# Three blocks of 384 tokens in tiles of 128 instead of four of 288 in tiles of 96, attention units in rings of their own, and the product with v by a block diagonal

## The chip, the cores and the metric

One core of one Trainium2 chip. The time is the device time of one execution, in microseconds (us); a kernel's time is the median of its runs. The engines are TensorE (PE, with its weight loads listed apart as PEld), VectorE (DVE), ScalarE (ACT), GpSimd (POOL) and SyncE (SP), which here only issues DMAs.

## The reference

A vision tower of depth 1 on 32 images of 3 x 96 x 96: 36 patches an image, so 1,152 tokens of 192 features.

```python
h = tok(x)                                  # patches -> 5 mixtures of channels -> 192 features, plus biases
h = h + attn(layernorm(h), W_qkv, W_out)    # 12 heads of 64 within an image; logits are q k * 8
h = h + ffn(layernorm(h), gate, w1, b1, w2, b2)
# ffn: argmax over 8 experts; out = gelu(xt @ w1[e] + b1[e]) @ w2[e] + b2[e], hidden size 768
```

All is fp32 in and out. The choice of the expert depends on the exact logits of the gate, so the kernel splits factors of q, k and v into a high and a low part in fp32r.

## The kernel before

**Tiling.** The 1,152 tokens go in NB = 4 blocks of BT = 288, each of NT = 3 tiles of TT = 96. A unit of attention is two images, GT = 72 tokens, so a block has NU = 4 units and starts and ends on whole images: block, tile group and unit never cross. Everything indexed by block, `h`, `qT`, `kT`, `probs`, `rows`, `v`, is a buffer for one block.

**Stages of a block b** (PE's program, `body`, which handles the tokens of b + 1 between the attention of b): `tokens` (the six products of x with the effective patch weights, a tile at a time; L413), `turn_xn` (two transposes of the normalised tile; L421, L422), `heads` (q and k of a pair of heads for the whole block, five products of 128 weight columns by 288 tokens; L428), `values` (v of a tile, two halves of 384 columns, five products each with the tokens stationary; L428), `scores` (24 small products for a unit; L458), `turn_probs` (24 small products with the identity; L472), `attend` (probabilities with v, 24 products of 36 x 64 weights by 36 columns; L487), `project` (output projection of a tile; L498), `gate` (L513, L514), `ranks` (L529 to L538: place of each token among those of its expert), and at the end `first_lists` and `more_lists`, which turn the ranks into lists of token numbers. Fp32 products are two instructions each, fp32r ones a single one; `keep_clock` (L556) are filler transposes.

**Softmax of a unit.** `scores` fills two PSUM banks, which it waits for until DVE has run `soften` of the unit before (maximum, L1027, subtraction, L1028); ACT takes the exponential (L840); DVE runs `normalise` (sum, reciprocal, product; L1036 to L1038); PE turns the probabilities (`turn_probs`), ACT copies them out of PSUM (`take_probs`, L857, one copy), PE runs `attend`, ACT copies the result (`take_attended`, L863). `turn_probs(g + 1)` waits for the copy of g, `attend(g)` too. DVE's order is written out in `soften_all` and `body`.

**v.** ACT copies a tile's values to SBUF, SP moves them by DMA (L382) to partitions 0 to 35 for one image of a unit and 64 to 99 for the other; a run of tokens that lies in one image and one tile is one DMA, 40 in all.

**Order around it.** PE, ACT and DVE each have an order written out by hand; PSUM banks 0 to 3 are a ring of results of `heads`, `values`, `tokens`, `project` and the transposes, whose order stands in `OPENING`, `MIDDLE` and `FINAL`. The last block overlaps with nothing: its four units' attention, three projections, gates and ranks stand in a row, and behind them the lists, the gather of the tokens, and the experts: 16 tiles of 128 gathered tokens, `up` (L738, L744), `down` (L764). SP loads x block by block into `xb`, all of w1 at once, and w2 in three pieces of experts.

## Time and profile before

| | |
|---|---|
| median of 3 runs | 268.12 us (265.56 to 268.46) |
| the profiled execution | 268.89 us, span 267.0 |
| PE busy | 253.0 us, 95% |
| PE weight loads | 235.1 us, 88% |
| DVE, ACT, POOL busy | 131.2, 114.7, 55.8 us |
| mean granted clock of TensorE | 0.974 |

Busy time of PE counts overlapped matmuls once, and their listed durations reach from issue to the modelled end: the cost of one is the step to the next start. The span is the time from the first instruction to the last on the core; the device time lies 1.9 us above it.

### The profile page before, as it was taken

Reading aid. Unit: us, or ns where it says so; the run is one execution under the profiler, and the core shown is the slowest. Engines: PE = TensorE matmul, PEld = TensorE weight load, DVE = VectorE, ACT = ScalarE, POOL = GpSimd, SP = SyncE. Lnnn points to the kernel's source line nnn. Section 1 sums busy time; section 2 is a strip of 40 time slices with the busy share of each in tenths; the row PEclk is TensorE's granted clock in tenths of the full one; section 3 lists DMA queues with packets and bytes.
Section 4 is the critical chain, followed back from the end, with each engine's and each line's share of the span. In section 5 each row is a group of like instructions: output and inputs, shape, how many; then the busy total and the mean of one; then the engine's idle time right before and its main releaser. Section 6 shows DMA issues by size and latency. Waiting matters only on the chain.

```text
span 267.0 us, 9115 instructions
## 1 busy us (share of the span) xinstructions
PE 253.0 (95%) x3855; PEld 235.1 (88%) x3855; DVE 131.2 (49%) x422; ACT 114.7 (43%) x309; POOL 55.8 (21%) x97
## 2 busy tenths in 40 slices
PE   7999999999999999989999989889999999999990
PEld 6999889999899999779999879888899999999990
DVE  3786387331596731786731793267242423232310
ACT  2866552525343525432525443240342547475420
POOL 3020002122002122002124000125234444443222
PEclk9999999999999999999999975999999999999997
DMA  6939982313631306421005411022211211222000
GB/s 227 310 103 305 433 294 72 101 39 99 239 87 49 136 2 178 189 60 47 6 0 184 124 48 49 1 69 62 87 35 52 72 63 61 62 53 68 3 3 0
DMA packets 8019, 27.17 MB, mean 102 GB/s; under 512 B 2085, under 2 KB 3777, under 8 KB 7468
## 3 DMA queue, kind: packets, MB, share of 16 engines
q1 hardware_dynamic: 5820, 22.02, 25.1%
q0 software_dynamic: 1840, 4.13, 5.7%
q8 instruction: 31, 0.51, 0.8%
q10 hardware_dynamic: 320, 0.44, 0.6%
q14 instruction: 8, 0.07, 0.1%
HBM read 20.40 MB, written 3.34 MB: 89 GB/s over the span
## 4 chain that ended last, share of the span: by engine, by line
PE 90%; DVE 5%; issue 2%; ACT 1%; POOL 1%; POOLq 0%; DVEq 0%
PE psum L428 20%; PE psum L764 12%; PE psum L498 10%; PE psum L738 8%; PE psum L413 7%; PE psum L472 6%; PE psum L487 5%; PE psum L744 5%; PE psum L556 3%; PE psum L458 3%; PE psum L584 2%; PE psum L567 2%; PE psum L727 2%; PE psum L421 1%; PE psum L514 1%
## 5 line engine op out<-in xcount | busy, mean ns | idle before, releaser
L428 PE MATMUL psum<-xn_hi,wq_parts 128*128 128x288 f32 x144 | 34.4, 308 | 0.3 <-DVE late_r L1004 0.3
L764 PE MATMUL psum<-w2s,kT 128*128 128x192 f32 (+1 forms) x192 | 33.8, 327 | 0.0
L1344 POOL TENSOR_SCALAR veps<-mv 96x1 f32<-96x1 f32 x21 | 4.6, 217 | 133.3 <-DVE mv L985 133.3
L764 PEld LDWEIGHTS psum<-w2s,kT 128*128 128x128 f32 x192 | 30.8, 190 | 0.1
L428 PE MATMUL psum<-late_r,wq_parts 128*128 128x288 f32 x96 | 27.4, 294 | 0.0
L498 PE MATMUL psum<-wo,oT 128*96 128x192 f32 x144 | 27.1, 340 | 0.0
L1403 POOL DMA_INDIRECT out<-oT,ids x16 | 16.2, 1010 | 43.7 <-DVE oT L1300 43.7
L428 PEld LDWEIGHTS psum<-xn_hi,wq_parts 128*128 128x128 f32 x144 | 24.4, 188 | 0.5 <-ACT xn_hi L826 0.5
L960 ACT ACTIVATE kT<-psum,w1s 128x128 f32<-128x128 f32 x48 | 13.3, 375 | 26.3 <-PE psum L744 26.3
L498 PEld LDWEIGHTS psum<-wo,oT 128*96 128x96 f32 x144 | 23.6, 171 | 0.5
L428 PE MATMUL psum<-wq_parts,xn_hi 128*96 128x384 f32 x72 | 22.2, 363 | 0.0
L1282 DVE COPY qT<-psum 128x128 f32<-128x128 f32 x16 | 4.7, 292 | 34.5 <-PE psum L728 34.5
L960 ACT ACTIVATE kT<-psum,late 128x128 f32<-128x128 f32 x48 | 13.3, 376 | 16.7 <-PE psum L744 11.2
L472 PEld LDWEIGHTS psum<-ident,kT 36*36 36x36 f32 x768 | 16.1, 122 | 3.7 <-DVE kT L1038 1.7
L848 ACT COPY wq_in<-psum 96x384 f32<-96x384 f32 x24 | 11.3, 473 | 17.8 <-PE psum L428 17.8
L413 PE MATMUL psum<-late,xb 128*96 128x192 f32 x108 | 18.8, 329 | 0.0
L472 PE MATMUL psum<-ident,kT 36*36 36x36 f32 x768 | 17.9, 206 | 0.8 <-DVE kT L1038 0.8
L428 PEld LDWEIGHTS psum<-late_r,wq_parts 128*128 128x128 f32 x96 | 18.1, 188 | 0.0
L1392 POOL DMA_INDIRECT xb<-token_table,ids x16 | 15.6, 976 | 9.9 <-DVE ids L1222 5.3
L413 PEld LDWEIGHTS psum<-late,xb 128*96 128x96 f32 x108 | 17.2, 163 | 0.2
L835 ACT COPY kT<-psum 128x288 f32<-128x288 f32 x24 | 9.6, 400 | 16.8 <-PE psum L428 16.8
L487 PE MATMUL psum<-late 36*64 36x36 f32 x768 | 16.1, 233 | 0.7 <-issue 0.7
(165 smaller groups left out, 481.1 us busy)
## 6 DMA issues: line engine op xcount, KB each, us to landing
w1s<-w_b SPq DMA_DIRECT2D x1, 4632.0 KB, 18.2
xb<-xT SPq DMA_DIRECT2D x4, 864.0 KB, 5.7
w2s<-w SPq DMA_DIRECT2D x2, 1728.0 KB, 8.9
late<-wq_in SPq DMA_DIRECT2D x24, 108.0 KB
token_table<-rows SPq DMA_DIRECT2D x3, 432.0 KB, 3.3
w2s<-w SPq DMA_DIRECT2D x1, 1152.0 KB, 7.4
late<-w_proj SPq DMA_DIRECT2D x2, 480.0 KB, 3.9
b2s<-b SPq DMA_DIRECT2D x1, 768.0 KB
```

The costliest lines, as they stand in the source:

```text
L413: mm = pe.matmul(dst[0:TT, 0:D], xb[:, k, t * TT:(t + 1) * TT], weff[:, k // 2, k % 2, :], start=(k == 0), stop=(k == KX - 1))
L428: mm = pe.matmul(dst, lhsT, rhs, start=(i == 0), stop=(i == len(parts) - 1))
L472: mm = pe.matmul(psum[image, TR_BANK, cols], probs[image, g, cols], ident[image, image], start=True, stop=True)
L487: mm = pe.matmul(psum[DH * k:DH * (k + 1), SIDE_BANKS[i], at:at + PER_IMAGE], v[image, g, col:col + DH], probsT[image, g % 2, j * PER_IMAG ...
L498: mm = pe.matmul(dst[0:TT, 0:D], oT[:, c, t * TT:(t + 1) * TT], wo[:, c, :], start=(c == 0), stop=(c == PAIRS - 1))
L738: pe.matmul(psum[:, 2 * p2 + c % 2, at:at + SLOT], w[:, c * P:(c + 1) * P], fxA[p2], start=(c < 2), stop=False)
L744: mm = pe.matmul(psum[:, 2 * p2 + c % 2, at:at + SLOT], w[half, FF + at:FF + at + P], fxB[p2][half, :], start=False, stop=(c >= FCH - 2))
L764: mm = pe.matmul(psum[:, Y_BANKS[j % 2], 0:D], hidT[j % 2][:, c * P:(c + 1) * P], w[:, :, c, :], start=(c == 0), stop=(c == FCH - 1))
L848: cp = act.copy(v_tiles[:, t, f * (HD // 2):(f + 1) * (HD // 2)], acc(slot[0])[0:TT, 0:HD // 2])
L960: ge = act.activation(hidT[p2][:, c * P:(c + 1) * P], psum[:, 2 * p2 + c % 2, c // 2 * P:(c // 2 + 1) * P], ACT.Gelu, bias=w1_of(j)[:, UP ...
L1392: pool.indirect_dma_start(out=xg[j % 4], out_offset=None, in_=table, in_offset=bass.IndirectOffsetOnAxis(ap=ids[:, j:j + 1], axis=0)).then ...
L1403: pool.indirect_dma_start(out=out, out_offset=bass.IndirectOffsetOnAxis(ap=ids[:, j:j + 1], axis=0), in_=yo[j % 4], in_offset=None, bounds ...
```

## The change

**Blocks.** `NB` is 3, `TT` 128: a block has 384 tokens in three tiles, nine tiles in all (`TILES`), and its product for q and k has 384 columns. 384 is not a multiple of 72, so a unit, an output row tile and a block no longer coincide. Units run from 0 to 15 through the kernel; a block has 5, 5 and 6 of them (`UNITS`), and finishes the row tiles whose last unit it has: 2, 3 and 4 (`GROUPS`). Their buffers become rings: `v` of 6 units, `probs` of 4, `h` of 7 tiles (which makes `hres`, the copy kept for the residual, superfluous), `rows` and what turns it of 4 tiles. `qT` and `kT` hold 432 tokens, so that from block 1 on a q or k product is copied in two pieces.

**Product with v.** The turned probabilities of a unit's two images are laid into a block diagonal of 100 partitions by 12 x 72 columns, whose other blocks POOL sets to zero once (together with the gap between the images in `v`). One product of all 100 partitions then serves both images. It goes into the ring of banks 0 to 3, no longer into the banks of the scores. ACT copies the probabilities in two pieces, one for each image.

**Order.** `PRODUCTS` lists all results in one row. The last block is written out anew: its six units' scores, softmax, turning and products with v stand between its own values. Every middle stage of scores has five units, the fifth behind the last value product. **Memory and DMA.** x lies in the place of w1's experts 6 and 7, which are loaded after the last block of x; the effective patch weights, the low parts and one block diagonal lie in w2's experts 5 to 7, so w2 comes in four pieces. x comes by tiles. POOL's indirect warm-up goes to `bias`. Before the experts, the transpose of the second gathered tile moves ahead of `up(0)`.

```diff
-NB = 4
+NB = 3
-TT = 96
+TT = 128
-NU = BT // GT
+NU = TOKENS // GT
-W2_PIECES = [slice(0, 3), slice(3, 6), slice(6, EXPERTS)]
+W2_PIECES = [slice(0, 3), slice(3, 5), slice(5, 7), slice(7, EXPERTS)]
+V_SLOTS, P_SLOTS, H_SLOTS, ROW_SLOTS = 6, 4, 7, 4
+UNITS = [range(b * BT // GT, (b + 1) * BT // GT) for b in range(NB)]
+GROUPS = [[t for t in range(TILES) if last_unit(t) in units] for units in UNITS]
...
+            def attend(u):
+                slot = product("at", u)
+                dst = into(slot)
+                pe.wait_ge(tr_free, u + 2)
+                values_here(pe, u)
                 for c in range(PAIRS):
                     for k in range(2):
-                        for i in range(GROUP):
-                            image = slice(HALF * i, HALF * i + PER_IMAGE)
-                            mm = pe.matmul(psum[DH * k:DH * (k + 1), SIDE_BANKS[i], at:at + PER_IMAGE],
-                                           v[image, g, col:col + DH],
-                                           probsT[image, g % 2, j * PER_IMAGE:(j + 1) * PER_IMAGE],
+                        j = 2 * c + k
+                        mm = pe.matmul(dst[DH * k:DH * (k + 1), c * GT:(c + 1) * GT],
+                                       v[0:SPAN, u % V_SLOTS, j * DH:(j + 1) * DH],
+                                       probsT[u % 2][:, j * GT:(j + 1) * GT],
                                            start=True, stop=True)
...
+            def take_probs(u):
+                act.wait_ge(tr_full, u + 1)
+                for i in range(GROUP):
+                    keys = slice(HALF * i, HALF * i + PER_IMAGE)
+                    dst = probsT[u % 2][keys, :].rearrange("p (c k m n) -> p m k c n", c=PAIRS, k=2, m=GROUP)
+                    cp = act.copy(dst[:, i, :, :, :],
+                                  psum[keys, TR_BANK, 0:WIDTH].rearrange("p (k c n) -> p k c n", k=2, c=PAIRS))
+                cp.then_inc(tr_free, 1)
...
+            def values_and_scores(b):
...
                 turn_probs(u)
                 scores(u + 3)
                 values(t + 2, 1)
+                scores(u + 4)
...
+            def last_block(b):
+                u, t, r = UNITS[b][0], NT * b, GROUPS[b][0]
+                values(t, 0)
+                all_taken(pe, queries(b))
+                scores(u)
+                values(t, 1)
+                scores(u + 1)
+                values(t + 1, 0)
+                scores(u + 2)
+                values(t + 1, 1)
+                turn_probs(u)
+                ranks(b - 1)
+                scores(u + 3)
+                values(t + 2, 0)
+                turn_probs(u + 1)
+                attend(u)
+                scores(u + 4)
+                values(t + 2, 1)
+                turn_probs(u + 2)
+                attend(u + 1)
+                scores(u + 5)
+                project(r)
+                turn_probs(u + 3)
+                attend(u + 2)
+                turn_probs(u + 4)
+                attend(u + 3)
+                project(r + 1)
+                turn_probs(u + 5)
+                attend(u + 4)
+                turn_rows(r)
+                attend(u + 5)
+                project(r + 2)
+                turn_rows(r + 1)
+                project(r + 3)
+                gate(b, 0, 2, False)
...
+            for blocks in probsT:
+                own(pool.memset(blocks, 0.0))
+            own(pool.memset(late[HALF // 2:HALF, 2 * REPR * D:v_cols], 0.0))
...
             turn_x(0)
             keep_clock(6, TR_BANK)
+            turn_x(1)
             up(0, more_lists)
```

In the last block DVE runs soften(u), soften(u + 1), normalise(u), soften(u + 2), normalise(u + 1), soften(u + 3), normalise(u + 2), then the placing of the tokens of the block before, then soften(u + 4), normalise(u + 3), soften(u + 5), normalise(u + 4), normalise(u + 5).

## Rows read from the trace of the kernel before

**Rows 1.** The page, part 1: busy us (share of the span) x instructions, each engine.

```profile
PE 253.0 (95%) x3855; PEld 235.1 (88%) x3855; DVE 131.2 (49%) x422; ACT 114.7 (43%) x309; POOL 55.8 (21%) x97
```

**Rows 2.** Windows by stage: length, busy us (instructions) of engines, PEclk, DMA share, GB/s.

```profile
0.00:39.80 39.80, 37.21 (x449) 33.73 (x449) 25.68 (x55) 23.28 (x53) 4.41 (x19) 1.00 0.80 279
39.80:78.40 38.60, 38.60 (x774) 36.05 (x774) 20.30 (x64) 16.06 (x45) 5.34 (x13) 1.00 0.34 110
78.40:118.30 39.90, 38.67 (x772) 35.93 (x771) 23.65 (x80) 16.34 (x45) 5.33 (x13) 1.00 0.34 104
...
157.40:167.60 10.20, 10.20 (x209) 9.22 (x207) 5.09 (x21) 3.52 (x7) 0.00 (x0) 0.50 0.12 32
```

**Rows 3.** The chain that ended last, in order of time: start us, us, what.

```profile
54.59 2.12 PE psum L498 x12
...
58.90 1.95 PE psum L498 x12
...
64.53 2.02 PE psum L428 x15
...
66.91 0.27 PE psum L513 x2
...
72.19 0.58 PE psum L458 x47
...
82.28 0.92 PE psum L472 x45
...
83.24 0.70 PE psum L487 x46
...
193.35 1.95 PE psum L764 x12
```

**Rows 4.** Groups by line and shape: out<-in, shape, xcount | busy us, mean ns | idle.

```profile
L764 PEld LDWEIGHTS psum<-w2s,kT 128*128 128x128 f32 x192 | 30.8, 190 | 0.1
...
L498 PE MATMUL psum<-wo,oT 128*96 128x192 f32 x144 | 27.1, 340 | 0.0
...
L428 PE MATMUL psum<-wq_parts,xn_hi 128*96 128x384 f32 x72 | 22.2, 363 | 0.0
...
L413 PE MATMUL psum<-late,xb 128*96 128x192 f32 x108 | 18.8, 329 | 0.0
...
L857 ACT COPY late<-psum 100x432 f32<-100x432 f32 x16 | 8.3, 518 | 13.2 <-PE psum L472 13.2
...
L513 PEld LDWEIGHTS psum<-gwA,xrA 128*96 128x96 f32 x24 | 3.1, 161 | 0.3 <-ACT xrB L897 0.2
```

**Rows 5.** Timeline of PE, values of one tile: start us, us, engine, line.

```profile
71.15 0.34 PE L428 MATMUL psum<-wq_parts,xn_hi 128*96 128x384 f32 x1
...
71.85 0.34 PE L428 MATMUL psum<-wq_parts,late_r 128*96 128x384 f32 x1
```

**Rows 6.** Timelines of DVE and PE at the end of block 0's scores.

```profile
75.39 0.60 DVE L1027 TENSOR_REDUCE top<-psum 100x12 f32<-100x432 f32 x1
...
77.97 0.60 DVE L1036 TENSOR_REDUCE total<-kT 100x12 f32<-100x432 f32 x1
...
78.22 1.30 PE L413 MATMUL psum<-late,xb 128*96 128x192 f32 x7
```

**Rows 7.** Timeline and chain of PE in the last block, and the second up projection.

```profile
156.41 1.03 PE L472 MATMUL psum<-ident,kT 36*36 36x36 f32 x48 [0.77 <-DVE kT L1038]
...
164.88 3.49 PE psum L498 x12
...
190.50 0.71 PE L738 MATMUL psum<-qT,w1s 128*128 128x128 f32 x4 [0.44 <-DVE qT L1284]
```

**Rows 8.** Timelines of POOL and SP in the opening; the DMAs of v in one block.

```profile
1.97 0.41 POOL L1332 MEMSET zeros<- 1x384 f32 x1
...
9.15 0.29 SPq L365 DMA_DIRECT2D token_table<-zeros  x1
...
L382 SPq DMA_DIRECT2D late<-wq_in x8: 713/714/1378, 72.0 to 79.0; - x8
```

More of the change, by code:

```diff
@@ new lines @@
+PRODUCTS = [("bias",)] + [("tok", t) for t in range(NT)] + [("xt", t) for t in range(NT)] + queries(0) + values_of(0)
+for b in range(NB - 1):
+    PRODUCTS += middle(b) + (values_of(b + 1) if b + 1 < NB - 1 else [])
+PRODUCTS += values_of(NB - 1)[0:5] + [("at", U0)] + values_of(NB - 1)[5:] + [
+    ("at", U0 + 1), ("o", O0), ("at", U0 + 2), ("at", U0 + 3), ("o", O0 + 1), ("at", U0 + 4), ("gt", O0),
+    ("at", U0 + 5), ("o", O0 + 2), ("gt", O0 + 1), ("o", O0 + 3), ("gt", O0 + 2), ("gt", O0 + 3)]
@@ L109, in image_runs, with runs_to, held @@
     return found
-RUNS = [image_runs(t) for t in range(NT)]
-RUNS_OF = [sum(run[2] == g for runs in RUNS for run in runs) for g in range(NU)]
+RUNS = [image_runs(t) for t in range(TILES)]
+def runs_to(u):
+    return sum(run[2] % V_SLOTS == u % V_SLOTS and run[2] <= u for runs in RUNS for run in runs)
+def held(b):
+    found, tok = [], b * BT
+    while tok < (b + 1) * BT:
+        n = min(HELD - tok % HELD, (b + 1) * BT - tok)
+        found.append((slice(tok % HELD, tok % HELD + n), slice(tok - b * BT, tok - b * BT + n)))
+        tok += n
+    return found
 def build(nc, xT, w_proj, reps, b_proj, w_qkv, w_out, gate_w, gate_b, w1_b1, w2, b2, out):
@@ L560, in _ @@
             keep_clock(14, SMALL_BANK)
-            slot = product(("bias",), 0, opening=True)
+            slot = product("bias")
             dst = into(slot)
@@ L594, in _ @@
             pe.wait_ge(wq_split, 2)
-            all_taken(pe, [("xt", t) for t in range(NT)], 0, opening=True)
+            all_taken(pe, [("xt", t) for t in range(NT)])
             for n, key in enumerate(QK):
@@ L795, in _ @@
                 if c == 2:
-                    slot = product(("bias",), 0, opening=True)
+                    slot = product("bias")
                     complete(act, slot)
@@ L813, in _ @@
             for t in range(NT):
[L814 removed]
+                slot = product("tok", t)
                 complete(act, slot)
@@ L842, in take, with exponentials @@
-            def take(w, c, slot):
-                (take_q if w == "q" else take_k)(c, slot)
-            def take_v(t, f, slot):
-                complete(act, slot)
-                cp = act.copy(v_tiles[:, t, f * (HD // 2):(f + 1) * (HD // 2)], acc(slot[0])[0:TT, 0:HD // 2])
+                for to, tokens in held(b):
+                    cp = act.copy((qT if w == "q" else kT)[:, c, to], acc(slot[0])[:, tokens])
+                cp.then_inc(free[slot[0]], 1)
+            def exponentials(u):
+                act.wait_ge(sc_free, u + 2)
+                act.activation(probs[:, u % P_SLOTS, :], probs[:, u % P_SLOTS, :], ACT.Exp,
+                               scale=LOGIT_SCALE).then_inc(exp_ready, 1)
@@ new lines, in take_o, with finish_row @@
+            def take_o(t):
+                slot, i = product("o", t), t - GROUPS[block_of(t)][0]
+                complete(dve, slot)
+                dve.tensor_tensor(rows[:, i, 0:D], acc(slot[0])[0:TT, 0:D], h[:, t % H_SLOTS, :],
+                                  ALU.add).then_inc(free[slot[0]], 1)
+                taken(dve, slot)
+                layernorm_stats(rows[:, i, 0:D], 1, i)
+            def finish_row(t):
+                i = t - GROUPS[block_of(t)][0]
+                normed(1, t)
+                layernorm(rows[:, i, D:2 * D], rows[:, i, 0:D], 1, i).then_inc(rows_ready, 1)
```

1051 lines of the change are left out of this document (534 added, 517 removed).

## The prediction

> **What bounds the kernel now.** I read the page first, then the windows by stage, the chain, the durations by shape and the timelines. TensorE (PE) is busy for 253 of 267 us [rows 1], and by stage it is full or nearly full in each block [rows 2]; the chain of waits runs along it, from product to product [rows 3]. So a change is worth what it takes from PE's queue, less any wait that it puts there. Since matmuls overlap, the cost of one is the step from start to start, not its listed duration: three projections for q and k take 2.02 us for 15 matmuls, 0.134 us each, and one output projection 1.95 us for 12 instructions, 0.163 us each [rows 3]. A matmul on fp32 is two instructions, on fp32r one [rows 4].
>
> **What the change takes from PE.** A tile has 128 tokens instead of 96, so a matmul whose stationary side is a tile of tokens does a third more in the same step.
>
> - Values: 12 tiles x 2 x 5 = 120 matmuls become 90. Their step is 0.175 us [rows 5]: -5.2.
> - Tokens outside the opening: 9 x 6 x 2 = 108 instructions [rows 4] become 6 x 12 = 72, still 192 columns, 0.163 us [rows 3]: -5.9. The opening has three tiles either way.
> - Output projection: 144 [rows 4] become 108: -5.9.
> - q and k: here tokens are the moving side, the columns stay 69,120. 240 matmuls of 0.134 = 32.2 become 180 of 384 columns, which step like the values, 0.175 = 31.5: -0.7.
> - Gate: a tile costs 0.53 us (four instructions, two in 0.27 [rows 3]), set by the weight load, since 8 columns move; a 128-column load takes 190 ns where 96 take 161 [rows 4], so 12 x 0.53 = 6.4 become 9 x 0.61 = 5.5: -0.9.
> - Transposes and ranks: fewer, wider: -0.6.
>
> Together -19.2 us. The scores and the turning of the probabilities keep their instructions, 0.58 and 0.92 us a unit [rows 3], over 16 units in all.
>
> **The product with v** halves its instructions, 48 to 24 a unit, of 72 columns over 100 partitions instead of 36 over 36. Before, row halves and column halves of the array work at once: 0.70 us a unit [rows 3]. Afterwards each instruction takes all rows, and only the column halves can go abreast. A column of fp32 costs 0.163/192 = 0.85 ns, so 72 are 61 ns. If the two halves run fully abreast, a unit takes 24 x 0.031 = 0.73; if they follow one another, 24 x 0.061 = 1.47. The nearest row is that of the scores: 36-column moves in 64-row halves, 24 to each half, done in 0.58 us. One after the other they would need 24 x 0.031 = 0.74 in each half, so column halves on the same rows do overlap. I take 0.80, plus 0.15 for the changes between halves and the whole array: a projection behind a half-array unit took 2.12 instead of 1.95 us [rows 3]. That is 0.95, or +0.25 x 16 = +4.0; bounds +0.5 (fully abreast, and no time lost in changes) to +14.7 (one after the other, with them).
>
> One rule speaks against this. The Trainium skill (TensorE: Matmul & The Clock Gate, Part 3, The mechanism) has weight loads overlap matmuls in flight only when the row group differs, which would leave each load of the new product exposed. The trace does not bear its narrow form out: the down projection loads the same rows every time, 190 ns a load [rows 4], and still steps at 1.95/12 = 0.163 us [rows 3]. By the row the sum keeps +4.0, by the rule it gets the +46 of the slower rival below.
>
> **What it adds to the waits.**
>
> - *Scores.* The fifth unit's scores now stand ahead of the next block's tokens and need the scores bank, free once DVE has subtracted the maximum of the fourth (soften). DVE takes 2.6 us for a soften and a normalise, some 1.2 and 1.4 [rows 6]. In the stage of before that ends at 78.2, where PE turns to the tokens, the third normalise starts at 77.97 [rows 6]; now the fourth soften stands there and ends at 79.2, and with the semaphore PE waits about 1.1 us. In the opening and in block 1: +2.2.
> - *Copies of the probabilities.* One ACT copy of 432 elements, 0.52 us [rows 4], becomes two of 36 partitions, still 432 elements each: 1.04. PE's next unit waits for it. Between two units lie a product with v and a transpose, 1.15 us, against 1.04 plus about 0.3 of semaphores on both sides: 0.3 at the third unit, 0.4 at the last, where nothing but a product stands between. +0.7 in each of two middle blocks, +0.7 in the last: +2.1. Elsewhere a projection or tokens (1.95) cover it. On ACT the copies add 8.3 us in all to 115 busy, with its other work falling.
> - *Last block.* Six units' softmax chains at 2.6 us [rows 6] instead of four, with the placing of the last block's tokens among them, which delays soften(u + 4). With values, scores and transposes laid out by their steps, PE waits 0.5, 0.5 and 0.9 us; before 0.77 [rows 7]: +1.1.
> - *After the last projection.* Two gates instead of one precede the end of the gates (+0.5, and 0.3 for the copies of the fourth tile), and DVE takes logits, levels and at_rank for four tiles instead of three, a third more of some 3 us: +1.8. The transpose of the second gathered tile moves ahead of the first up projection, whose successor no longer waits 0.44 us for DVE [rows 7]: -0.4. +1.4.
> - *One block less.* Block 0 took 38.6 us [rows 2]. Its parts by their steps are 37.3: three token tiles and three projections at 1.95, 12 products for q and k at 0.67, six of values at 0.93, four units at 0.58 + 0.95 + 0.70, gate 1.6, ranks 0.5, transposes 1.0. That leaves 1.3 of changes of shape and small waits; block 1 had 1.3 more. One such block goes, with the mean of 1.3 and 2.6: -1.9.
>
> Sum +4.9 us.
>
> **At nothing, with their cover.** The memsets of the block diagonals on POOL (some 4,400 more elements on a lane, about 4.7 us at 0.41 for 384 [rows 8]) end near 7.5; SP, which waits for them, comes to that wait at 9.15 [rows 8], and POOL has nothing else until the first layernorm. The first tokens are 288 KB more, 1.0 us at the opening's 279 GB/s [rows 2], behind which PE has the bias's products; without that cover +1.0. The split copies of q and k cost ACT about 0.65 us for every 0.87 on PE. SP's queue: v goes out in 40 DMAs, as before, 13 a block instead of 10, at 0.71 us [rows 8]; the copies for the last tile end about 16 us into the last block and are read at 24. The two late experts of w1, the last of w2 and the tokens by thirds stand on SP between these, tens of us before their readers; were this wrong, the third expert piece would hold up the 39 filler transposes ahead of the experts. The experts themselves (16 x 4.5 us from 187 on) are untouched. Dropping hres takes a copy off POOL, which idles.
>
> **The clock.** In the profiled run the granted clock was 0.50, 1.2 GHz, from 157.4 to 167.6 [rows 2], after a stretch in which PE had scores, turned probabilities and the 0.77 us wait for DVE. A projection took 3.49 there instead of 1.95 [rows 7]. PE was busy throughout, so half of the 10.2 us, 5.1, was lost. The new last block spreads value products through the softmax, which are full-array work: if the clock holds there, -5.1; if it falls as before, nothing.
>
> **Sum.** -19.2 + 4.0 + 4.9 = -10.3 with the fall, -15.4 without. The profiled execution took 268.9 us, its span 267.0; the median of the runs, 268.1, is 0.8 lower, and I leave that out. So 253.5 without a fall, 258.6 with one; I predict 253.5.
>
> **The rivals.**
>
> 1. *The clock falls in the last block all the same.* Against it the values; for it the waits of 0.5 to 0.9 us, with scores, turning and products with v about them, quite as before 157.4. 258.6 us. Chance 0.27.
> 2. *Column halves do not go abreast once an instruction has all rows.* 1.47 + 0.15 a unit, +14.7 instead of +4.0: 264 us, or 269 with a fall. The scores speak against it, though their rows are halves. Chance 0.12.
> 3. *The waits are hidden*: POOL, ACT and DVE have slack, and a softmax ahead of time would take most of the +4.9 and of the product's 0.25. 246 to 249 us. Chance 0.12.
> 4. *Slower than before: weight loads of the product with v are exposed*, as the Trainium skill's rule would have it. In the gate, where nothing hides a load, an instruction takes 0.27/2 = 0.13 us for 96 columns of weights [rows 3]; two thirds of it for the product's 64 columns, 0.09, and 0.06 to move make 0.15 each, 3.6 us a unit: +46 against 0.70 instead of +4, 295 us. It turns the result from about 1.1 us above what I take, 2.1 us a unit. Chance 0.04. With a late v, which would stall PE at each product of the last block for about 2 us (a DMA's landing), 6 x 2 = 12: 266 us; chance 0.03.
> 5. *The change does nothing for PE*, because steps of 128-wide tiles are longer: the down projection with 128 rows at 0.163 excludes it for tokens and output. Chance under 0.01.
>
> The forecast itself has 0.41. Its own range is 249 to 257. From 246 to 261 the hidden waits, the forecast and the fall are in, 0.8 together. Below about 1% no change can be told from none here; faster by more holds all but the exposed loads and the worst of rival 2 with a fall: 0.93, within 1% 0.03, slower 0.04.
>
> **What would show it.** The product with v: 0.8 to 1.0 us a unit in the chain. Fewer instructions by the counts above, at 0.163 and 0.175. q and k at 0.175 for 384 columns. Waits of PE for DVE's soften before each fifth scores, and for ACT's copy of the probabilities in the last two units. Last block (first value product to last projection) near 32 us without a fall, 28.1 before. The forecast is wrong if 384-column products step above 0.18, if a unit's product passes 1.2, or if PE waits for v or x.

## The result, and the profile after

The changed kernel takes 251.63 us in the median (250.81 to 253.8), the kernel before 268.12 in the same comparison: a ratio of 0.945, 95% interval 0.940 to 0.950. The prediction was 253.5, with a range of its own of 249 to 257. The profiled execution took 253.8 us, its span 252.1; it is the longest of the five. The profiled execution of the kernel before (268.9 us, mean granted clock 0.974) was one of its slow ones, and the part on the clock below says what that does to the reading.

The page's part 1 after, which answers to [rows 1]: busy us (share of the span) x instructions.

```profile
PE 234.9 (93%) x3271; PEld 218.2 (87%) x3271; DVE 119.4 (47%) x364; ACT 119.0 (47%) x318; POOL 52.9 (21%) x84
```

PE has 584 instructions fewer and is busy 18.1 us less, while the span is 14.9 us shorter: PE still is the bound, with 3 us more of idle time (17.2 for 14.0). The windows by stage, as in [rows 2] (length, busy us (instructions) of PE, PEld, DVE, ACT and POOL, granted clock, DMA share, GB/s); block 0 starts with its first tokens at 46.8, the last block's values at 125.3, and its last projection ends at 157.2.

```profile
0.00:46.80 46.80, 41.57 (x497) 38.36 (x497) 27.68 (x58) 26.18 (x55) 7.84 (x21) 0.96 0.73 233
46.80:90.30 43.50, 42.20 (x775) 39.02 (x774) 21.08 (x62) 22.49 (x63) 3.95 (x10) 1.00 0.34 107
90.30:125.30 35.00, 34.72 (x469) 33.02 (x469) 15.70 (x57) 16.27 (x52) 6.04 (x13) 1.00 0.31 101
125.30:157.20 31.90, 30.87 (x814) 27.32 (x813) 21.93 (x63) 16.33 (x37) 2.38 (x6) 1.00 0.33 96
157.20:175.70 18.50, 15.75 (x143) 14.56 (x142) 11.55 (x56) 2.84 (x7) 5.75 (x7) 0.91 0.29 92
11.61:15.03 3.42, 3.42 (x13) 3.42 (x12) 2.04 (x4) 3.02 (x6) 0.00 (x0) 0.50 1.08 223
165.21:168.63 3.42, 3.42 (x18) 3.42 (x17) 3.11 (x16) 0.00 (x0) 2.02 (x2) 0.50 0.13 30
```

A block of 384 tokens takes 43.5 us where one of 288 took 38.6 [rows 2]: 0.113 us a token instead of 0.134. The whole stretch of the blocks is at a granted clock of 1.00. The two stretches at half clock (1.2 GHz) lie outside it, in the opening and behind the last projection; a third begins at 250.55, at the very end of the kernel. The chain of waits (start us, us, what) has the same steps as [rows 3], at the new size:

```profile
44.91 0.62 DVE kT L1171
45.53 0.04 issue
45.57 0.65 PE psum L537 x47
...
50.95 0.96 PE psum L551 x48
51.91 0.90 PE psum L564 x24
...
59.30 2.15 PE psum L577 x12
...
68.91 2.64 PE psum L505 x15
...
155.20 1.95 PE psum L577 x12
...
164.91 5.98 PE psum L633 x39
```

L505 is q, k and v (here 15 products for q and k of 384 columns, 0.176 each; the 384 columns of [rows 5] had 0.175), L537 the scores, L551 the turning of the probabilities, L564 the product with v, 0.90 us a unit, L577 the output projection, L633 the fillers. The first lines show the wait that the fifth unit's scores bring: the subtraction on DVE (L1171) ends at 45.53, and only then PE goes on. PE's waits, summed (line, releaser, us in total, times, longest):

```profile
PE psum L537 <- DVE kT L1171: 2.7, 6, 0.9
...
PE psum L647 <- DMA bp<-b_proj: 1.6, 1, 1.6
...
PE psum L564 <- issue: 0.6, 2, 0.3
...
PE psum L551 <- ACT w2s L957: 0.3, 1, 0.3
```

To compare executions I cut the span in four: the opening up to the first product for q and k; the blocks, from there to the start of the last projection's last product; the tail, from there to the first up projection; and the rest, the experts. The kernel before has 21.7, 153.0, 12.4 and 79.9 us, the changed one 24.4, 132.5, 16.2 and 79.1. So the blocks gain 20.6 us, and the opening and the tail give 6.5 of them back; the up projection, whose successor no longer waits for DVE [rows 7], returns 0.8.

### The profile page after: what moved, and what is told of

It is laid out like the page before. It is cut to its first block, busy times and chain, and to the rows that moved or that the text cites. A ratio compares the mean times of both kernels' runs of the same rounds, so it can differ in the third digit from the quotient of the medians.

```text
span 252.1 us, 7816 instructions
## 1 busy us (share of the span) xinstructions
PE 234.9 (93%) x3271; PEld 218.2 (87%) x3271; DVE 119.4 (47%) x364; ACT 119.0 (47%) x318; POOL 52.9 (21%) x84
## 4 chain that ended last, share of the span: by engine, by line
PE 80%; DVE 10%; DMA 2%; ACT 2%; issue 2%; SPq 1%; POOL 0%; DVEq 0%; POOLq 0%; ACTq 0%
PE psum L505 16%; PE psum L859 12%; PE psum L831 9%; PE psum L577 8%; PE psum L837 6%; PE psum L564 5%; PE psum L551 5%; PE psum L481 5%; PE psum L633 3%; PE psum L537 2%; DMA bp<-b_proj 2%; PE psum L661 2%; DVE kT L1171 2%; DVE top L1170 2%; PE psum L820 2%
## 5 line engine op out<-in xcount | busy, mean ns | idle before, releaser
L505 PE MATMUL psum<-xn_hi,wq_parts 128*128 128x384 f32 x108 | 31.8, 349 | 0.5 <-DVE w_r L1147 0.5
L1541 POOL DMA_INDIRECT out<-oT,ids x16 | 16.2, 1012 | 42.9 <-DVE oT L1464 42.9
L505 PE MATMUL psum<-w_r,wq_parts 128*128 128x384 f32 x72 | 24.2, 337 | 0.0
L505 PEld LDWEIGHTS psum<-xn_hi,wq_parts 128*128 128x128 f32 x108 | 19.9, 188 | 0.8 <-ACT xn_hi L923 0.7
L577 PE MATMUL psum<-wo,oT 128*128 128x192 f32 x108 | 19.8, 333 | 0.0
L1530 POOL DMA_INDIRECT wq_in<-token_table,ids x16 | 15.7, 982 | 13.6 <-DVE ids L1410 7.0
L551 PEld LDWEIGHTS psum<-ident,kT 36*36 36x36 f32 x768 | 14.8, 116 | 4.0 <-issue 3.2
L633 PE MATMUL psum<-ident 128*128 128x128 f32 x105 | 16.3, 316 | 1.8 <-POOL ident L1491 1.8
L577 PEld LDWEIGHTS psum<-wo,oT 128*128 128x128 f32 x108 | 17.4, 190 | 0.5
L551 PE MATMUL psum<-ident,kT 36*36 36x36 f32 x768 | 16.5, 200 | 0.5 <-ACT w2s L957 0.3
L505 PE MATMUL psum<-wq_parts,xn_hi 128*128 128x384 f32 x54 | 16.7, 363 | 0.0
L633 PEld LDWEIGHTS psum<-ident 128*128 128x128 f32 x105 | 14.5, 165 | 2.1 <-POOL ident L1491 1.8
L930 ACT COPY kT<-psum 128x384 f32<-128x384 f32 (+4 forms) x30 | 9.4, 354 | 11.5 <-PE psum L505 11.5
L930 ACT COPY qT<-psum 128x384 f32<-128x384 f32 (+4 forms) x30 | 9.4, 354 | 10.3 <-PE psum L505 10.3
L537 PEld LDWEIGHTS psum<-kT,qT 64*36 64x36 f32 x768 | 8.6, 113 | 6.0 <-DVE kT L1171 4.4
```

What stands on the lines that cost most here:

```text
L505: mm = pe.matmul(dst, lhsT, rhs, start=(i == 0), stop=(i == len(parts) - 1))
L537: mm = pe.matmul(psum[HALF * i:HALF * i + PER_IMAGE, SIDE_BANKS[k], c * PER_IMAGE:(c + 1) * PER_IMAGE], qT[heads_, c, t0:t0 + PER_IMAGE], ...
L551: mm = pe.matmul(psum[image, TR_BANK, cols], probs[image, u % P_SLOTS, cols], ident[image, image], start=True, stop=True)
L577: mm = pe.matmul(dst[0:TT, 0:D], oT[:, c, at:at + TT], wo[:, c, :], start=(c == 0), stop=(c == PAIRS - 1))
L633: pe.transpose(psum[:, bank, 0:P], ident[:, :], ident[:, :])
L930: cp = act.copy((qT if w == "q" else kT)[:, c, to], acc(slot[0])[:, tokens])
```

## The experiments

They ran in four groups (e0 to e3, e4 to e7, e8 to e10, e11), each beside the kernel before, which took 268.07, 267.24, 265.92 and 267.33 us in the median; a ratio is against that. The stretches are those of the profiled execution, in which the experts' part is 79.0 to 79.1 in every one but before. The half clock is what lies within the blocks. Of e10 only the time is used.

| kernel | median us | ratio (95%) | opening | blocks | tail | half clock in blocks | product with v, a unit |
|---|---|---|---|---|---|---|---|
| before | 268.12 | 1 | 21.7 | 153.0 | 12.4 | 10.2 | 0.70 |
| e0_after | 251.38 | 0.942 (0.936 to 0.949) | 22.1 | 132.3 | 15.2 | 0 | 0.90 |
| e1_halves | 259.75 | 0.966 (0.958 to 0.974) | 22.0 | 140.9 | 16.6 | 17.1 | 0.70 |
| e2_order | 258.77 | 0.966 (0.959 to 0.974) | 24.4 | 139.5 | 15.2 | 0 | 1.45 |
| e3_one_copy | 250.31 | 0.938 (0.933 to 0.942) | 22.4 | 131.4 | 16.1 | 0 | 0.90 |
| e4_bias_first | 251.93 | 0.948 (0.942 to 0.953) | 22.4 | 132.4 | 16.4 | 0 | 0.90 |
| e5_fifth_later | 250.34 | 0.941 (0.937 to 0.945) | 22.9 | 130.5 | 15.2 | 0 | 0.90 |
| e6_more_fillers | 251.85 | 0.946 (0.942 to 0.951) | 23.1 | 132.3 | 15.4 | 0 | 0.90 |
| e7_narrow | 263.73 | 0.991 (0.987 to 0.995) | 24.5 | 143.3 | 16.2 | 0 | 1.54 |
| e8_one_image | 252.04 | 0.943 (0.935 to 0.952) | 22.0 | 133.7 | 15.3 | 6.8 | 0.69 (half) |
| e9_values_together | 253.84 | 0.957 (0.953 to 0.960) | 21.9 | 135.0 | 15.0 | 3.4 | 0.90 |
| e10_three_together | 250.74 | 0.943 (0.938 to 0.947) | | | | | |
| e11_half_full_rows | 248.71 | 0.934 (0.927 to 0.940) | 22.5 | 130.0 | 15.5 | 0 | 0.82 (half) |

**e0_after** is the changed kernel once more. Its blocks agree with the first profile within 0.2 us, while opening and tail differ by 2.2 and 1.0: the blocks can be compared to some tenths of a us, the ends cannot.

> The changed kernel again, unaltered, as the measure for the runs beside it: a ratio of 0.945 to the kernel before, 251 to 254 us, the product with v at 0.90 us a unit in the chain.

**e1_halves: the product with v as before, in its own banks.** Its lines lie 5 to 9 further down (L556 turns, L571 is the product with v, L586 the projection).

```diff
-                        j = 2 * c + k
-                        mm = pe.matmul(dst[DH * k:DH * (k + 1), c * GT:(c + 1) * GT],
-                                       v[0:SPAN, u % V_SLOTS, j * DH:(j + 1) * DH],
-                                       probsT[u % 2][:, j * GT:(j + 1) * GT],
+                        col, j = (2 * c + k) * DH, k * PAIRS + c
+                        for i in range(GROUP):
+                            image = slice(HALF * i, HALF * i + PER_IMAGE)
+                            mm = pe.matmul(dst[i][DH * k:DH * (k + 1), c * PER_IMAGE:(c + 1) * PER_IMAGE],
+                                           v[image, u % V_SLOTS, col:col + DH],
+                                           probsT[u % 2][image, j * PER_IMAGE:(j + 1) * PER_IMAGE],
...
-                for i in range(GROUP):
-                    keys = slice(HALF * i, HALF * i + PER_IMAGE)
...
+                act.copy(probsT[u % 2][:, 0:WIDTH], psum[0:SPAN, TR_BANK, 0:WIDTH]).then_inc(tr_free, 1)
```

> The product with v back in its old form in an otherwise unchanged new kernel: 48 instructions a unit of 36 x 64 weights by 36 columns, image by image in the two row halves, each image into a bank of its own of the ring, and one copy of the probabilities instead of two. My theory: the unit goes back from 0.90 to 0.70 us (16 x 0.20 = 3.2) and the waits for the second copy go (2.1), less a little for the two banks and two copies of the result, so 4 to 5 us faster than the changed kernel, 247 to 248 us. The rival that these costs lie behind DVE's softmax anyway: within 1 us of the changed kernel.

I was wrong by 12 us. The product's 0.70 us is there (0.20 less a unit, 3.2 in all), and the kernel is 8 us slower. The chain in block 1, then PE's windows (length, busy us (instructions), granted clock, DMA share, GB/s):

```profile
98.19 0.73 PE psum L571 x48
98.92 2.15 PE psum L586 x12
...
103.07 0.62 PE psum L571 x27
103.69 0.88 issue
104.57 0.86 PE psum L571 x21
105.43 4.14 PE psum L586 x12
```

```profile
104.28:111.11 6.83, 6.54 (x39) 0.50 0.01 2
138.41:148.65 10.24, 10.01 (x197) 0.50 0.33 83
```

PE stops in the middle of a product, waiting for nothing that the profile shows ("issue"), and right behind it the clock is at half: a projection takes 4.14 us instead of 2.15. Such stops are 0.88, 0.50, 1.29 and 1.06 us long, 3.7 together; e0_after has none of this kind, only two of 0.28 between two products, which e3 below shows to be waits for the copy. 17.1 us at half clock cost about 8.3 us, since PE was busy for nearly all of it; with 2.8 us more of idle time and 2.4 us less for the products with v and the turning ahead of them, all by the starts of PE's instructions, this gives 8.7, and the blocks are 8.6 longer. The small products thus cost the clock and PE's flow of instructions, which I had priced at nothing. The split between the two is that of one execution: its mean granted clock is 0.939, the other five have 0.959 to 0.968 and take 256.5 to 260.5 us all the same.

The kernel before, which has the same small products, has two such stops as well, in the scores of block 1, and a clock of 1.00 around them [rows 2]:

```profile
112.89 0.31 issue
...
116.13 0.91 issue
```

What brings the clock down, the count of short instructions or the part of the array that they use, is what e7, e8 and e11 ask.

**e2_order: the same column half six times running** (k outside, c inside).

```diff
-                for c in range(PAIRS):
-                    for k in range(2):
+                for k in range(2):
+                    for c in range(PAIRS):
```

> Only the order of the 24 instructions of a product with v: first all six of one column half, then all six of the other, instead of in turn. If the cost of 0.90 us rests on the two column halves working abreast, a unit now takes 24 x 0.061 = 1.5 us and the kernel 16 x 0.6 = 9 to 10 us more, 261 to 263 us. The rival, that the order doesn't matter because each instruction is bound by its weight load or its issue: 0.90 us and no change.

In its chain:

```profile
51.97 1.45 PE psum L564 x24
```

In alternation it is 0.90. The starts of PE's instructions take this apart. Within one column half they lie 0.0625 us apart (0.061 in the prediction's serial case), in alternation 0.0315 on average: 24 of them start within 0.745 us. From the last start to that of the next product it is 0.155 us, in this kernel, the changed one, e1, e7, e8 and e11 alike. So column halves do run abreast, and nearly fully, though every instruction takes all 100 rows. The blocks are 7.1 us longer: 16 x 0.55 = 8.8, less the 0.9 us of waits for the copies, which the longer product hides; 0.8 us stay unexplained. The time, 258.8, is below the 261 to 263 expected.

**e3_one_copy: the copy of the second image's probabilities left out** (so its results in the product with v are not those of the unit).

```diff
-                for i in range(GROUP):
+                for i in range(1):
```

> Leaves out the copy of the second image's probabilities, so that half of every block diagonal stays zero; the products keep their size. It prices the second copy on ACT (0.51 us x 16). My theory: 1.5 to 2.1 us faster than the changed kernel (waits at the third and last unit of each middle block and at two of the last block), 249 to 250 us. The rival, that ACT is never late: within 0.5 us.

The blocks are 1.0 us shorter. The 0.28 us stops before the last product of a middle block and the 0.33 us wait for ACT in the last block are gone, and a stop of 0.3 has come. The two copies cost 1.0 us, half of what the prediction has.

**e4_bias_first: the bias is loaded ahead of x.**

```diff
+            sp.dma_start(bp[:, :], b_proj).then_inc(br_here, 16)
             for t in range(NT):
                 sp.dma_start(xb[:, t, :, :], xT[t]).then_inc(x_here, 16)
-            sp.dma_start(bp[:, :], b_proj).then_inc(br_here, 16)
```

> The transfer of the bias bp is issued ahead of the three transfers of x instead of behind them. Theory (the 288 KB more of x hold back a small transfer queued behind them, PE waits 1.58 us for it at L647, and the idle time lets the clock fall at 11.61 for 3.41 us): no wait for bp, no fall in the opening, the first statistics near 16.4 us where they were at 18.63, and 1.5 to 2.5 us less than the changed kernel, some 249.5 where both are timed. But x lands some 0.4 us later by it. Rival (the opening waits for x itself, and bp only happened to be named): within 0.5 us of the changed kernel.

No gain in time: 0.948 beside 0.942 and 0.945. Where the chain had the bias, it now has x:

```profile
3.54 6.88 DMA w1s<-xT
10.41 0.04 issue
10.46 0.66 PE psum L633 x4
```

The rival was right: everything issued there lands some 9.4 to 10.5 us into the span, and what PE wants first is late, by whichever name. Behind waits for the bias of 0.7 to 1.4 us (e1, e11, e3, e5, e6) the clock stayed up; behind 1.58, 1.61 and 1.75 (the changed kernel, e2, e7) the opening had 3.4 us at half clock and took 24.4 to 24.5 us instead of 22.0 to 23.1.

**e5_fifth_later: the fifth unit's scores behind the next block's first tokens.**

```diff
                 values(t + 2, 1)
-                scores(u + 4)
...
                 tokens(n)
+                scores(u + 4)
                 tokens(n + 1)
```

> In the two middle blocks the scores of the fifth unit are issued behind the next block's first tile of tokens instead of ahead of it. Theory (PE stands before them for VectorE's softmax of the third unit, 0.9 to 1.8 us a block, as the prediction has it): the waits of those two places go, and nothing is late behind, since the softmax of the fifth unit is wanted only three turns later: 1.5 to 2.5 us less than the changed kernel. Rival (VectorE is the bound of this stretch and PE only moves its wait to the turning of the first probabilities): within 0.5 us.

```profile
PE psum L537 <- DVE kT L1171: 1.0, 4, 0.3
```

The wait for soften has gone from 2.7 us in six places to 1.0 in four, and the blocks are 1.8 us shorter, with nothing late behind. In whole runs that is 0 to 1 us (0.941 beside 0.942 and 0.945), which this measurement can't tell from nothing, since the ends vary by more.

**e6_more_fillers: more fillers ahead of the last ranks and behind them.**

```diff
-                keep_clock(10, TR_BANK)
+                keep_clock(19, TR_BANK)
                 ranks(b)
...
-            keep_clock(6, TR_BANK)
+            keep_clock(9, TR_BANK)
             pe.wait_ge(at_rank_ready, 1)
```

> 19 filling products instead of 10 ahead of the last ranks and 9 instead of 6 behind them, so that PE is not idle while the queries' ranks are reckoned. Theory (the tail took 18.5 us for 15.45 because PE's idle time there lets the clock fall, and the fillers at half clock delay the first expert): no half clock behind the last projection, tail of 16 us, up to 2.5 us less. Rival (the fillers themselves are on the path, 9 at 0.14 us): up to 1 us more. Since the changed kernel was at half clock there for 6.8 us in one profile and 3.4 in another, the size may vary.

No gain in time. There is less half clock: the mean granted clock is 0.988 to 0.995 in all six executions, where e0_after has 0.981 to 0.983 in five of six. But the clock still fell behind the last projection, at 159.65, for 3.4 us, and PE no longer waits for DVE before the first up projection, but for the gather of its tokens:

```profile
165.95 1.17 POOL wq_in L1530
...
167.43 2.96 DMA wq_in<-token_table,ids
```

The tail, 15.4 us here and 15.2 in e0_after, has two chains of nearly one length: the fillers on PE, and DVE's ranks with the gather behind them.

**e7_narrow: all rows, but two instructions of 36 columns for one of 72.**

```diff
+                        for i in range(GROUP):
+                            lo, hi = i * PER_IMAGE, (i + 1) * PER_IMAGE
-                        mm = pe.matmul(dst[DH * k:DH * (k + 1), c * GT:(c + 1) * GT], ...
+                            mm = pe.matmul(dst[DH * k:DH * (k + 1), c * GT + lo:c * GT + hi], ...
```

> The block diagonal product as 48 instructions of 36 columns instead of 24 of 72, all 100 rows of the array as in the changed kernel. It tells what made e1_halves slower than the changed kernel: there a unit's product took 0.70 us against 0.90, as the prediction has it, but the span was 9.7 us longer, with 27.3 us at half clock against 6.8 and four stretches of 0.5 to 1.3 us in which PE waited for nothing but its own instructions (issue). Theory A (the count of short instructions does it: PE's instructions come too slowly, it stands still, and the clock falls): such idle stretches and falls here too, 4 us or more at half clock beyond the changed kernel, and a time of 255 to 262. Theory B (the half used rows of e1_halves do it): no falls in the blocks; the unit's product takes 0.9 to 1.5 us, the time is 251 to 260 by the product alone, clock near 0.98.

```profile
52.07 1.54 PE psum L566 x48
...
139.27 0.64 issue
```

The starts lie 0.029 us apart, a little under the serial rate of 36 columns (0.031); four instructions in a row go to the same half, where the changed kernel has two. That makes the product dearer than either theory had it, and the kernel too (263.7 for at most 262). The stops are there, 0.64, 0.37 and 0.53 us, as theory A wants, but the clock stays at 1.00 in all of the blocks, as B wants. 16 x 0.64 = 10.2 us for the product and 1.0 more of stops (1.5, for 0.6 in e0_after) make 11.2; the blocks are 11.0 longer. So stops come with the short instructions; they didn't bring the clock down here, but none is as long as the 0.88 and 1.29 us that stand right ahead of e1's two falls.

**e8_one_image: e1 with the second image's product left out, save one product, which is two instructions**, so 26 short ones a unit on 36 rows (the expectation counts 25).

```diff
-                        for i in range(GROUP):
+                        for i in range(GROUP if c == PAIRS - 1 and k == 1 else 1):
```

> As e1_halves, but the product with v of a unit's second image is left out, save one instruction: 25 instructions of 36 columns on 36 rows a unit, where e1_halves had 48. With the changed kernel (24 instructions on all rows, no fall in the blocks), e7_narrow (48 on all rows: stretches of idle 'issue' of 0.4 to 0.6 us, no fall in the blocks) and e1_halves (48 on 36 rows: issue 0.5 to 1.3 us and two falls in the blocks) it fills the fourth place. Theory A (many short instructions leave PE without instructions at times, and that idle time brings the clock down): no issue stretches over 0.4 us, no fall in the blocks, a unit's product 0.35 to 0.4 us, 242 to 246 us. Theory B (too little of the array is at work, whatever the count): the clock falls within the blocks though there are no issue stretches, 248 to 256 us.

```profile
96.56 0.69 PE psum L571 x24
...
142.30 0.89 PE psum L571 x25
143.20 3.83 PE psum L586 x12
```

```profile
143.19:146.61 3.42, 3.42 (x12) 0.50 0.01 2
150.02:153.44 3.42, 3.42 (x13) 0.50 0.58 175
```

The clock falls twice in the last block, with nearly as few instructions as in the changed kernel and stops of at most 0.6 us. That favours theory B. But e8 moves fewer columns too, and has a wait of 0.71 us for DVE at 135.9 that the changed kernel has not; e11 takes that apart. And a surprise: I had expected 0.35 to 0.4 us for half of the product, and it takes 0.69, as much as the whole. In e1 the two images' instructions ran side by side, on different rows; the halves of the columns alone give nothing below 0.029 us from start to start.

**e9_values_together: the last block's values no longer between all of its softmax.**

```diff
                 values(t, 1)
-                scores(u + 1)
                 values(t + 1, 0)
-                scores(u + 2)
+                scores(u + 1)
                 values(t + 1, 1)
+                values(t + 2, 0)
+                scores(u + 2)
+                values(t + 2, 1)
                 turn_probs(u)
                 ranks(b - 1)
                 scores(u + 3)
-                values(t + 2, 0)
                 turn_probs(u + 1)
                 attend(u)
                 scores(u + 4)
-                values(t + 2, 1)
```

> The last block's values are pulled out of the softmax of its units: two value products follow each other ahead of the scores of the second and third unit, and none stands behind the fourth. Theory (the values between the last units' softmax are what covers it, and what keeps the clock up in the last block, as the prediction has it): PE waits for VectorE or ScalarE 1 to 3 us more in the last block, and a fall of the clock moves into it, up to 3 us more; 253 to 257 us. Rival (the clock's level does not hang on the values, and the softmax has slack): within 1 us of the changed kernel, with the fall behind the last projection as before.

```profile
PE psum L537 <- DVE kT L1171: 3.5, 5, 1.4
...
PE psum L551 <- ACT late L957: 0.7, 1, 0.7
```

```profile
139.33:142.74 3.41, 3.41 (x49) 0.50 0.74 302
```

2.2 to 2.5 us slower by the medians, 3 to 4 by the ratios (0.957 beside 0.942 and 0.945), and the blocks are 2.6 us longer: waits of 0.69 and 1.38 us, and straight behind the second a stretch at half clock, which costs 1.7 us. All six executions have a lower mean clock (0.963 or 0.975) than any of the changed kernel (0.981 to 0.995). The values between the softmax thus cover it, and the clock holds with them, as the prediction has it. Whether it holds because they are full-array work or because PE isn't idle beside them, this run doesn't separate.

**e10_three_together: e4, e5 and e6 in one.**

> The edits of e4_bias_first, e5_fifth_later and e6_more_fillers together. Theory (each takes away a wait that is hidden or given back by itself, and only the fifth scores' are on the path): 249.5 to 250.5 us, as e5_fifth_later alone. Rival (with the bias first and the fillers more, the clock falls in fewer executions, so the median goes down further): 247 to 249.5 us.

250.74 us, as e5 alone. The two edits at the ends add nothing. No version that computes everything beat the changed kernel by more than the measurement can tell; e5, with the stretch of the blocks 1.8 us shorter, is the one to keep.

**e11_half_full_rows: e8's work, but on all rows.** One instruction of 36 columns for one of 72; the second image's product and the copy of its probabilities are left out, the first one's result stands in its place.

```diff
-                        mm = pe.matmul(dst[DH * k:DH * (k + 1), c * GT:(c + 1) * GT],
+                        mm = pe.matmul(dst[DH * k:DH * (k + 1), c * PER_IMAGE:(c + 1) * PER_IMAGE],
                                        v[0:SPAN, u % V_SLOTS, j * DH:(j + 1) * DH],
-                                       probsT[u % 2][:, j * GT:(j + 1) * GT],
+                                       probsT[u % 2][:, j * GT:j * GT + PER_IMAGE],
```

> 24 instructions a unit of 36 columns on all 100 rows; the product with v of a unit's second image and the copy of its probabilities are left out, and the first image's result is copied twice in its place. It differs from e8_one_image (25 instructions of 36 columns on 36 rows, two stretches at half clock in the last block) in the rows alone, and from the changed kernel in the columns moved. Theory B (few rows of the array at work bring the clock down): no half clock in the blocks, a unit's product 0.69 to 0.77 us, the stretch of the blocks 129 to 131 us, 247 to 250 us in all. Theory C (too few columns moved while the softmax is waited for, whatever the rows, and e8's wait of 0.7 us for DVE with it): a fall of the clock in the last block as in e8, the blocks 132 to 135 us.

PE's window over the last block, of e11 and then of e8:

```profile
120.50:153.00 32.50, 31.62 (x823) 1.00 0.33 98
```

```profile
120.50:153.00 32.50, 30.87 (x811) 0.90 0.31 93
```

Nearly the same number of instructions, of the same length, and the clock holds on 100 rows where it fell on 36. Between these profiles neither 24 or 48 instructions nor 36 or 72 columns decided, and theory B fits best. It isn't shown beyond doubt. The mean clock of e11's six executions is 0.981 to 0.988; that of e8's four is 0.965, 0.971, 0.977 and 0.983, and the one at 0.983 took 248.78 us, as e11 does: e8's falls do not come every time. PE also waited longer for DVE in e8's last block (0.71 us, for 0.32 in e11). And idle time brings the clock down as well, on all rows too, as e9 has it. How much of e1's half clock is due to its stops, and how much to its rows, stays open.

The time is as theory B has it (247 to 250), but a unit's product takes 0.82 us instead of 0.69 to 0.77. Half the columns take 0.82 where the whole takes 0.90: its cost is nearly all by the instruction, not by the columns.

## Why the prediction held, point by point

**The forecast and its time.** 253.5 was predicted, 251.63 measured, 1.9 less, within the range of 249 to 257 given for the likeliest case. By the profiled executions the sum was -15.4 and -15.1 came, but two misses cancel in that, which is luck: the blocks did 3.8 us better than the sum has them (-16.8 without the tail's +1.4; -20.6 measured), opening and tail 4.2 worse. Where the bias lands in time, as in e0_after, the ends are only 1 us worse, which goes some way to put the median below the forecast.

**What the change takes from PE (-19.2).** The steps are as taken: 0.176 us for 384 columns, 1.95 for a projection. The traces allow a direct account. I count PE's time in the blocks from each start to the next, with idle time over 0.25 us and the loss at half clock apart (us, before and e0_after):

| | before | e0_after | difference |
|---|---|---|---|
| q, k and values | 57.3 | 51.8 | -5.5 |
| tokens | 18.1 | 12.3 | -5.8 |
| output projection | 23.2 | 17.9 | -5.3 |
| scores, gates, ranks, other transposes | 19.7 | 16.9 | -2.8 |
| product with v and the turning ahead of it | 26.7 | 30.0 | +3.3 |
| idle over 0.25 | 3.0 | 3.4 | +0.4 |
| lost at half clock | 5.1 | 0 | -5.1 |

The first four make -19.4, where the prediction has -19.2. The product with v has +3.3 for +4.0, and the waits have +0.4 where the prediction's terms for the blocks (2.2 + 2.1 + 1.1 - 1.9) make +3.5. That is where nearly all of the blocks' 3.8 us come from.

**Product with v (+4.0, I took 0.80 + 0.15 a unit).** It is 0.90, and the projection behind it 2.15, as behind the old one 2.12 [rows 3]: +3.2 over 16 units. The bounds hold: 0.73 would be fully abreast, and the 24 starts take 0.745; e2 measured the other end, 1.45 instead of 1.47. The 0.155 us behind the last start is there in the old product too. The size was right, the picture less so: I reckoned by columns moved, and e11 takes 0.82 for half of them.

The Trainium skill (TensorE: Matmul & The Clock Gate, Part 3, The mechanism) has a weight load overlap matmuls in flight only where the row group differs. As the prediction used it, with every load exposed, it gives 3.6 us a unit; 0.90 refutes that. Yet between e1 and e8 it has a place: 48 instructions on alternating rows take 0.70 us, 26 on the same rows 0.69.

**Waits.** *Scores*, +2.2: two waits of 0.86 us came, and e5 took away 1.8. *Copies*, +2.1: e3 took away 1.0. The rows between a unit's turning and the next hid more of the second copy than I had laid out, in the middle blocks a stop of 0.28 each is all that is left. *Last block*, +1.1: waits of 0.28 and 0.28 for DVE (beside ACT's 0.33, which e3 has), less than the 0.77 of before [rows 7], so -0.2. *One block less*, -1.9: the kernel before had stops of 0.31 and 0.91 us in block 1 and of 0.69 in the last block (at 112.89, 116.13 and 169.21), 1.9 together, which are gone. The size is right; the prediction has it as a share of small losses, only part of which are these stops. In sum 1.7 + 0.9 - 0.2 - 1.9 came, and 3.5 was predicted. Rival 3, hidden waits, was thus half right: the waits are the mis-sized part of the sum.

**After the last projection, +1.4.** Up to the second up projection 15.5 us became 18.5. Gates and DVE's work for four tiles added 1.64 (1.8 predicted): the first logits come 1.17 later behind the last projection, at_rank 0.47 later still. The 39 fillers took 5.98 us instead of 4.32, +1.66, since the clock is at half from 165.2 to 168.6. That is the step that failed here: I had asked about the clock in the last block only. In e0_after the stretch is 17.6, 0.7 more than predicted, though it has 6.8 us at half clock, from 157.35 on: much of that only slows fillers in a time in which PE otherwise waits for DVE (1.20 and 0.42 us in the first profile, none here).

**At nothing: the first x.** This step failed. 288 KB more "behind which PE has the bias's products": those products themselves want the bias, which is queued behind x. PE waited 1.58 us for it, and the clock fell: first statistics at 18.63, and the opening 2.7 us longer. By e4, no order of the queue mends it. Without the fall (e0_after) it is 0.4 us, within the +1.0 named for a lost cover. v was never late, and no wait for the experts' pieces appears.

**The clock.** There is no fall in the blocks, in any of the profiles with the block diagonal and the values spread: between the two profiled executions -5.1 came as forecast, and rival 1 fell. For the medians it is worth less. The kernel before was run 50 times beside the experiments. In 18 of these the mean granted clock is 0.992 to 0.994. That is 3 to 4 us at half clock in all, and the profiled one has 3.8 us at the kernel's very end, so hardly any is left for the blocks; these 18 took 264.1 to 266.6 us, 265.2 in the middle. Thirteen have 0.974 or less, as the profiled one, and took 267.2 or more. So the long fall that the prediction prices is not the rule. Without it the kernel before is some 14 us slower than the changed one (251.4 and 251.6), where the prediction's sum without the clock has 10.3: from 265.2 that sum would have given 254.9. That is within the range as well, and its miss of 3 us is that of the waits and the product. The forecast came as near as it did because it started from an execution with the fall and took the fall off.

The reason given was only half of it, too. I gave the values as the cause; e9 bears them out, and e1 shows that the block diagonal, which the prediction has as a cost of 4 us, is needed as well: without it the values alone don't hold the clock, and the kernel loses 8 us, part of it in stops. That it is the rows of the product that matter is what e8 against e11 speaks for.

**Rivals.** 2 (halves not abreast, 264) is excluded by 0.90 against e2's 1.45; e2 itself came to 258.8. 4 is excluded by the same row, and its late v by its absence from PE's waits. 5 falls with the counts and the table. Of the signs named, the last block is 31.9 us for 32, a unit's product is inside 0.8 to 1.0, and the wait for ACT's copy came once, with 0.33 us. PE waited for neither v nor x in the changed kernel's profiles, but for the bias, which no sign named.

## What to carry to other kernels

Price an edit to PE's instructions not only by their steps but by what they do to the clock of the stretch: here a product that costs 0.2 us more a unit, with twice the columns on all rows, saved 8 us, by the clock and by PE's stops together. Before a stretch at half clock is priced, compare the mean granted clock of the profiled execution with those of the others: here only a quarter of them had so low a clock. In these runs, small instructions on part of the array were cheap only as long as the clock held and the instructions kept coming. Measure stretches between two events of the kernel (here the blocks) rather than the whole, when its ends vary by more than the edit is worth.

## What the hardware showed unexpectedly

- The step from start to start of fp32 instructions with 64 weight columns: 72 columns on 100 rows, 0.0625 us where the column half stays (e2) and 0.0315 where it alternates (e0); 36 columns on 100 rows 0.029, in both e11 (the half changes every second instruction) and e7 (every fourth); 36 on the 36 rows of one image 0.029 too (e8); 36 on 36 rows, both images' rows in turn, about 0.0145 (e1). Changing rows halves the time; changing column halves helps the long instruction and not the short one. A floor of about 0.03 us for each instruction on the same rows fits all of these; what sets it wasn't measured.
- A product of half-array instructions and one of whole ones both leave 0.15 us from their last start to the next product's first (before, e0, e1, e7, e8, e11), and an output projection right behind either has a longer first step, 0.24 to 0.27 us for 0.163.
- PE stood still for 0.3 to 1.3 us in the middle of runs of short instructions (the kernel before, e1, e3, e7, e8), waiting for nothing that the profile shows. With 24 instructions in the product there was none in e0 and e11, and one of 0.32 us in e3. That instructions came too slowly is a possible cause; it stays open.
- The same program had a stretch at half clock in its opening in one profile and none in another, with a transfer that landed 0.5 us later in the first.
